# Two causal attentions in 64-row tiles with keys kept twice, and two narrow cross attentions on the halves of the rows

## What is computed

```python
# layer 0, stage l0a: 16 heads of width 8, causal
s = q @ k.T * 8 ** -0.5; s = where(key <= query, s, -big); y = softmax(s) @ v
# layer 1, stage l1a: 16 heads of width 64 on a latent of 32 values per token, causal
q_latent = (x Wq Wk_up.T) * 64 ** -0.5; s = q_latent @ latent.T; y = softmax(masked s) @ latent @ Wv_up @ Wout
# layers 2 and 3, stages l2x and l3x: 16 heads of width 8 over the 77 context tokens
s = q @ k.T * 8 ** -0.5; s = clip(s, -10000, 10000) in layer 2 only; y = softmax(s) @ v
```

## Time and profile before

| what | value |
|---|---|
| runs of the kernel before | 1514.69, 1516.36, 1518.23 us (median 1516.36) |
| profiled execution | 1514.06 us |
| its span, first to last instruction | 1512.2 us |
| mean granted clock of TensorE | 0.979 |
| VectorE, ScalarE, GpSimd busy | 63%, 45%, 23% of the span |
| DMA | 79.13 MB |

### The profile page before, as it was taken

How to read it: one execution, slowest core, us unless ns; L and a number is a source line. 1 busy time by engine, 2 the same in 40 slices (tenths; PEclk the granted TensorE clock), 3 DMA queues, 4 the chain that set the end, 5 groups by cost and what they waited for, 6 DMA issues and landing times. The chain is left out here.

```text
span 1512.2 us, 27644 instructions
## 1 busy us (share of the span) xinstructions
PE 1418.1 (94%) x10790; PEld 890.2 (59%) x10790; DVE 955.7 (63%) x1911; ACT 674.3 (45%) x1651; POOL 346.3 (23%) x372
## 2 busy tenths in 40 slices
PE   8999999999999998998998988989998999999996
PEld 6665574644666656566786857674444555664434
DVE  6676372644366655645668337668888887677755
ACT  4776244324267654524420324533556777750002
POOL 4000031100101010010421202027777665600001
PEclk9999899999899999999999999999999999999998
DMA  3000000421000000000011302010110101399980
GB/s 126 2 2 2 3 2 0 154 72 42 15 2 2 2 2 17 1 20 4 2 60 78 126 11 83 2 43 15 42 42 28 30 15 26 64 223 254 253 213 15
DMA packets 24062, 79.13 MB, mean 52 GB/s; under 512 B 4808, under 2 KB 6646, under 8 KB 23552
## 3 DMA queue, kind: packets, MB, share of 16 engines
q1 hardware_dynamic: 23072, 74.26, 18.0%
q10 hardware_dynamic: 864, 3.15, 0.8%
HBM read 72.11 MB, written 1.08 MB: 48 GB/s over the span
## 5 line engine op out<-in xcount | busy, mean ns | idle before, releaser
L193 PE MATMUL psum<-ident 128*128 128x128 f32 x1392 | 175.7, 284 | 13.0 <-DVE var L143 5.6
L193 PEld LDWEIGHTS psum<-ident 128*128 128x128 f32 x1392 | 167.4, 198 | 20.9 <-DVE var L143 6.6
L475 ACT ACTIVATE pt<-psum,quad_max 128x128 f32<-128x128 f32 (+3 forms) x256 | 133.6, 525 | 68.4 <-DVE quad_max L513 64.4
L184 POOL TENSOR_TENSOR rstd<-var,minus_half 128x4 f32<-128x4 f32 x30 | 30.7, 1023 | 574.5 <-DVE var L143 539.4
L513 DVE TENSOR_REDUCE quad_max<-psum 128x1 f32<-128x128 f32 (+3 forms) x256 | 113.5, 485 | 67.7 <-PE psum L404 67.4
L2733 PE MATMUL psum<-pt,slots 128*128 128x512 f32 x256 | 115.0, 604 | 3.5 <-DVE pt L2886 2.9
L2712 PE MATMUL psum<-slots,xn_t 128*128 128x512 f32 x256 | 113.9, 605 | 3.1 <-DVEq L2857 3.1
L2471 ACT ACTIVATE p<-psum,duo_max 128x512 f32<-128x512 f32 x128 | 86.9, 683 | 43.2 <-DVE duo_max L2506 43.1
L2801 ACT ACTIVATE pt<-psum,p 128x64 f32<-128x64 f32 x256 | 58.0, 393 | 72.5 <-POOL wide L2943 43.7
L2733 PEld LDWEIGHTS psum<-pt,slots 128*128 128x128 f32 x256 | 48.0, 192 | 69.6 <-issue 50.8
L2506 DVE TENSOR_REDUCE duo_max<-psum 128x1 f32<-128x512 f32 x128 | 82.3, 684 | 10.0 <-PE psum L2382 7.8
(11 more groups left out here) (505 smaller groups left out, 2794.1 us busy)
## 6 DMA issues: line engine op xcount, KB each, us to landing
pt<-scratch_out_gates SPq DMA_DIRECT2D x32, 256.0 KB, 12.2
heads<-scratch_out_gates SPq DMA_DIRECT2D x24, 256.0 KB, 14.5
slots<-in_s_l0f SPq DMA_DIRECT2D x8, 514.0 KB, 3.3
wide<-scratch_gates SPq DMA_DIRECT2D x8, 512.0 KB, 7.5
slots<-in_s_l3v SPq DMA_DIRECT2D x8, 512.0 KB, 3.3
context_v<-scratch_out_gates SPq DMA_DIRECT2D x16, 256.0 KB, 18.3
slots<-in_s_l3o ACTq DMA_DIRECT2D x6, 512.0 KB, 10.2
weights<-in_w_l1a SPq DMA_DIRECT2D x1, 2624.0 KB, 9.4
```

What stands on the lines that cost most here:

```text
L193: nc.tensor.matmul(m.ps[bank][:, 0:P], m.ident[:, :], m.ident[:, :], start=True, stop=True, skip_group_check=True)
L475: nc.scalar.activation(m.quad_p[:, i % 2, g, 0:keys], m.ps[g][:, 0:keys], ACT.Exp, bias=m.quad_max[:, i % 2, g:g + 1], accum_out=sum_colum ...
```

## The change

In both causal attentions:

- The keys (l0a) or latents (l1a) are kept twice, in one copy with zeros in the odd groups of 32 rows and in the other with zeros in the even ones. ScalarE writes the first copy and then VectorE the second from the same bank. Scores become matmuls over 64 rows: head place g takes the rows of half g % 2 and the copy g // 2, so the heads are in the order 0, 2, 1, 3 (`HEAD_OF`).
- The mask becomes, for each head, two bf16 matmuls over 64 rows with 64 columns each.
- The turns are in halves: rows 0 to 63 of four heads and two key blocks go to one bank, rows 64 to 127 to another. Per pair of key blocks there are two banks, VectorE copies the first and ScalarE the second. A set of 1 to 4 blocks thus uses 2, 2, 4, 4 banks, where it used 1, 2, 3, 4.
- TensorE's order becomes: scores of set i (heads 2, 3); turn of the first pair of blocks of set i - 1, after all four exponentials; scores of set i + 1 (0, 1); turn of the second pair of blocks, if there is one; values of set i - 2. VectorE's copies move likewise.

In both narrow crosses the scores are matmuls over 64 rows with `keys_own` twice as wide (616 columns to build instead of 308), and the eight transposes become sixteen halves.

Three constants are added (`later`, `parity`, `rows8`), so three DMAs and one cast on ScalarE. The core of the diff:

```diff
 def quad_scores(...):
-    for g in heads:
-        nc.tensor.matmul(m.ps[g][:, keys - P:keys], m.ident_bf[:, :], m.future_bf[:, :], start=False,
-                         stop=True).then_inc(m.quad_scores, 1)
+    for part in range(2):
+        for g in heads:
+            own, at = half_rows(g % 2), keys - P + 64 * part
+            last = nc.tensor.matmul(m.ps[g][:, at:at + 64], m.later_bf[own, part, :], m.ident_bf[own, own], start=False,
+                                    stop=part == 1)
+            if part == 1:
+                last.then_inc(m.quad_scores, 1)
+
+def quad_turn(nc, pe, m, a, n, pair):
+    banks = [turn_bank(pe, m, a.turn[n, 2 * pair + half]) for half in range(2)]
+    blocks = pair_keys(n, pair)
+    for kt in blocks:
+        for g in range(GROUP):
+            for half in range(2):
+                own, at = half_rows(half), (kt % 2 * GROUP + g) * 64
+                last = nc.tensor.transpose(banks[half][:, at:at + 64], m.quad_p[own, n % 2, g, kt * P:(kt + 1) * P],
+                                           m.ident[own, own])
+                if kt == blocks[-1] and g == GROUP - 1:
+                    last.then_inc(m.quad_turned, 1)
 
 def quad_tensor(...):
-            for kt in range(n % NQ + 1):
-                bank = turn_bank(pe, m, a.turn[n, kt])
-                for g in range(GROUP):
-                    if kt == 0:
-                        pe.wait_ge(m.quad_exp, GROUP * (a.sets0 + n) + g + 1)
-                    last = nc.tensor.transpose(bank[:, g * P:(g + 1) * P], m.quad_p[:, n % 2, g, kt * P:(kt + 1) * P],
-                                               m.ident[:, :])
-                last.then_inc(m.quad_turned, 1)
+            pe.wait_ge(m.quad_exp, GROUP * (a.sets0 + n) + GROUP)
+            quad_turn(nc, pe, m, a, n, 0)
         if i + 1 < SETS:
             quad_scores(nc, pe, m, a, i + 1, (0, 1), q, k, q_ready)
+        if 0 <= n < SETS and key_pairs(n) > 1:
+            quad_turn(nc, pe, m, a, n, 1)
...
+def quad_take(copy, eng, m, a, n, u):
+    pair, half = divmod(u, 2)
+    blocks = pair_keys(n, pair)
...
+    copy(m.quad_pt[:, n % 2, blocks[0]:blocks[-1] + 1, :].rearrange("p k (g a q) -> p (k g) a q", a=2, q=64)[:, :, half, :],
+         bank[:, 0:len(blocks) * S // 2].rearrange("p (k q) -> p k q", q=64)).then_inc(m.quad_taken[a.turn[n, u][0]], 1)
...
 def quad_vector(...):
-            for kt in range(0, n % NQ + 1, 2):
-                quad_take(nc.vector.tensor_copy, dve, m, a, n, kt)
+            quad_take(nc.vector.tensor_copy, dve, m, a, n, 0)
         if i + 1 < SETS:
             maxima(i + 1, (0, 1))
+        if 0 <= n < SETS and key_pairs(n) > 1:
+            quad_take(nc.vector.tensor_copy, dve, m, a, n, 2)
...
 def l0_attn_tensor(nc, pe, m):
-                q=lambda g, b, j, qt: m.head_qs[own(g), j, b * S + qt * P:b * S + (qt + 1) * P],
-                k=lambda g, b, keys: m.k_t[own(g), b * S:b * S + keys],
+                q=lambda g, b, j, qt: m.head_qs[half_rows(g % 2), j, b * S + qt * P:b * S + (qt + 1) * P],
+                k=lambda g, b, keys: m.head_keys[g // 2][half_rows(g % 2), b * S:b * S + keys],
...
 def l0_attn_vector(nc, dve, m):
     head_queries(0)
+    for j in range(2):
+        copied(m, dve, f"l0k{j}")
+        bank = read(m, dve, f"l0k{j}", 1)
+        nc.vector.tensor_scalar(m.head_keys[1][:, j * S:(j + 1) * S], bank[:, :], m.parity[:, 1:2], w["bk_odd"], ALU.mult,
+                                ALU.add).then_inc(emptied(m, f"l0k{j}"), 1)
...
 narrow_cross, tensor:
                 for x in range(2):
-                    rows = own(2 * half + x)
+                    rows = slice(64 * x, 64 * x + 64)
                     last = nc.tensor.matmul(m.ps[2 * (k % 2) + x][:, 0:GROUP * SC], m.q_t[rows, b * S + qt * P:b * S + (qt + 1) * P],
-                                            m.keys_own[rows, b, 0:GROUP * SC], start=True, stop=True)
+                                            m.keys_own[rows, b, half * GROUP * SC:(half + 1) * GROUP * SC], start=True, stop=True)
...
                 for h in range(8):
-                    last = nc.tensor.transpose(m.ps[4 + h // 4][0:SC, (h % 4) * P:(h % 4 + 1) * P],
-                                               m.xp[:, n % XP_BUFFERS, h * SC:(h + 1) * SC], m.ident[:, :])
+                    for low in range(2):
+                        rows = slice(64 * low, 64 * low + 64)
+                        last = nc.tensor.transpose(m.ps[4 + low][0:SC, h * 64:(h + 1) * 64],
+                                                   m.xp[rows, n % XP_BUFFERS, h * SC:(h + 1) * SC], m.ident[rows, rows])
```

More of the change, by code:

```diff
@@ L357, in __init__ @@
             if 0 <= i - 1 < SETS:
-                for kt in range((i - 1) % NQ + 1):
-                    use(self.turn, (i - 1, kt))
+                for u in range(2 * key_pairs(i - 1)):
+                    use(self.turn, (i - 1, u))
             if self.ends_group(i - 2):
@@ L373, in all_taken @@
         for bank in range(len(T_BANKS)):
-            last = max((u for (k, kt), (b, u, _) in self.turn.items() if k == n and b == bank), default=None)
+            last = max((uses for (k, _), (b, uses, _) in self.turn.items() if k == n and b == bank), default=None)
             if last is not None:
@@ L380, in quad_set, with key_pairs, pair_keys @@
     return n // (NQ * GROUP), n // NQ % GROUP, n % NQ
+def key_pairs(n):
+    return n % NQ // 2 + 1
+def pair_keys(n, pair):
+    return range(2 * pair, min(2 * pair + 2, n % NQ + 1))
 def turn_bank(pe, m, use):
@@ L466, in quad_scalar @@
         n = i - 1
-        taken = [kt for kt in range(n % NQ + 1) if kt % 2 == 1] if 0 <= n < SETS else []
+        taken = [2 * pair + 1 for pair in range(key_pairs(n))] if 0 <= n < SETS else []
         if i < SETS:
@@ L485, in quad_scalar @@
             take_output((i - 3) // a.group_sets)
-        for kt in taken:
-            quad_take(copy, act, m, a, n, kt)
+        for u in taken:
+            quad_take(copy, act, m, a, n, u)
 def quad_gpsimd(nc, pool, m, a, groups, shares, output):
@@ L548, in l0_attn_tensor @@
             nc.tensor.matmul(bank[:, :], wt, m.xn_t[:, j * S:(j + 1) * S], start=True,
-                             stop=True).then_inc(filled(m, f"{name}{j}"), 1)
+                             stop=True).then_inc(filled(m, f"{name}{j}"), 2 if name == "l0k" else 1)
     tokens_tensor(nc, pe, m, "l0v", m.xn_t, w["wv"])
-    pe.wait_ge(m.consts_cast, 2)
-    for name in ("l0q", "l0k"):
-        for j in range(2):
-            copied(m, pe, f"{name}{j}")
+    pe.wait_ge(m.consts_cast, 3)
+    for j in range(2):
+        copied(m, pe, f"l0q{j}")
+        copied(m, pe, f"l0k{j}", 1)
     def ramp(i):
@@ L1189, in l1_attn_tensor @@
     keep_busy(nc, m, 5)
-    for name in ("l1al0", "l1al1", "l1at0", "l1aq0"):
+    for j in range(2):
+        copied(m, pe, f"l1al{j}", 1)
+    for name in ("l1at0", "l1aq0"):
         copied(m, pe, name)
@@ L1242, in l1_attn_vector @@
     norm_to_turn(nc, dve, m)
+    for j in range(2):
+        copied(m, dve, f"l1al{j}")
+        bank = read(m, dve, f"l1al{j}", 1)
+        nc.vector.tensor_scalar(m.latent_t[1][:, j * S:(j + 1) * S], bank, m.parity[:, 1:2], None,
+                                ALU.mult).then_inc(emptied(m, f"l1al{j}"), 1)
     bank = read(m, dve, "l1at0")
@@ L2972, in run @@
             item(m, f"{name}{n}", 6 + n % 2)
-    for name in ("l0n", "l0q", "l0k", "l0v"):
+    for name in ("l0n", "l0q"):
         pair(name)
+    for j in range(2):
+        item(m, f"l0k{j}", 6 + j, 2)
+    pair("l0v")
     for b in range(B):
@@ L2990, in plan @@
     run("l1an", 2)
-    run("l1al", 2)
+    for j in range(2):
+        item(m, f"l1al{j}", 6 + j, 2)
     run("l1at", 1)
@@ L3090, in build @@
         m.pair_rope = heads[:, :, :].rearrange("p (s w) n -> p s w n", w=2)
-        m.latent_t = m.keys_own[:, 0, 0:T]
+        m.latent_t = [m.keys_own[:, par, 0:T] for par in range(2)]
+        m.head_keys = [m.k_t[:, :], m.wide[:, 0, :]]
         m.slots_all = sb("slots", [P, 2 * SLOT_W])
@@ L3498, in constants @@
         "future": np.where(np.arange(P)[None, :] > np.arange(P)[:, None], np.float32(-BIG), np.float32(0)),
+        "later": np.where((64 * np.arange(2)[None, :, None] + np.arange(P)[:, None, None] % 64) > np.arange(P)[None, None, :],
+                          np.float32(-BIG), np.float32(0)).reshape(P, 2 * P),
+        "parity": (np.arange(P)[:, None] // 32 % 2 == np.arange(2)[None, :]).astype(np.float32),
         "rows4": quarter * np.float32((P // H) ** -0.5),
+        "rows8": np.concatenate([quarter * (np.arange(P)[:, None] // 32 % 2 == odd) for odd in range(2)],
+                                axis=1).astype(np.float32) * np.float32((P // H) ** -0.5),
         "cols4": np.ascontiguousarray(np.broadcast_to(quarter.T[None], (P, GROUP, P))),
```

81 lines of the change are left out of this document (52 added, 29 removed).

## The result

The changed kernel takes 1498.93 us (median of four runs, 1496.50 to 1500.74) beside 1516.59 for the kernel before on the same chip: a ratio of 0.988, 95% interval 0.986 to 0.990, or -17.7 us. The forecast was -32 (1484, range 1454 to 1504): right in sign and inside its range, but nearly twice the gain. The profiled execution took 1497.48 us (span 1495.7), so -16.6 between the two traces.

The account below looks back on a forecast made before the run. TensorE's instruction stream was taken as the bound: attentions -27, starts +1.4, drains +0.6, last cross -6.0, layer 2's cross -2.2, wider keys +1.3, together -32 us from 1516.36, so 1484, range 1454 to 1504.

Parts of the forecast that it names:

- its three waits: Causal attentions, per cycle: TensorE waits 1.3 us (third tile's turn, VectorE's copy), 0.35 (fourth tile's turn), 0.45 (ScalarE's last exponential).
- The sum for a cycle: Causal attentions, four query tiles: TensorE's scores 4.27, masks 1.09, half transposes 2.72, values 2.76 plus 0.60, before waits.
- starts: Start of each causal attention: keys written twice, so the value projection begins one pass later, +0.7 us each.
- drains: Ends of the causal attentions: the halves wait for one more copy, +0.6 us in all.
- the pairs: Last narrow cross: a pair of steps falls from 5.90 to 5.04 us, 7 of 8 pairs, -6.0 us.
- the wider keys: Before both narrow crosses: masked keys twice as wide, 0.65 us more each, +1.3 in all.
- The first one: Narrow cross in layer 2, which also clips: 0.32 us saved a pair, -2.2 us over 7, before the wider keys.
- the falling clock as a rival: Causal attentions: TensorE's idle time lowers its clock; near 1600 us throughout, 1540 for half the cycles; chance 5%.
- Not held up: Rival, causal attentions: maxima and copies overlap better, a cycle is 11.4 to 12 us, kernel 1460; chance 20%.
- bind fully: Rival, causal attentions: other engines make each half cycle wait, 14.5 us a cycle, kernel 1499; chance 12%.
- (b): Causal attentions, turning the fourth tile: TensorE waits for the copy of the first part's bank, 0.35 us a cycle.
- Nothing gained: Rival: a half transpose costs 0.053 to 0.062 us instead of 0.034, kernel within 4 us of 1516; chance 3%.

Follow-up runs that it names:

- the two second traces: The kernel before and the changed kernel, each profiled once more without any edit: 1514.66 and 1500.37 us.

## Why the prediction was right, and where its sizes were off

**TensorE's instruction stream was the bound, and the other engines come last after it.** Right: the cycle, its three waits, their order and their releasers came out as walked through. The sum for a cycle was 11.4 + 2.1; it measured 11.8 + 2.09. The 0.4 is where the sum was mis-sized, and it cost 15 x 0.4 = 6 us; it is what is left of errors that partly cancel (score pairs +0.73, halves +0.26, values +0.04, masks with the entries into values -0.67). I had put the whole 0.21 us of a score pair that no column explains on the change of shape. A pair of 64 rows among 64-row tiles still has a part of it: 61.79 - 61.51 = 0.28 us at 128 columns, where the slope alone gives 0.213. That is 0.07 us that no column explains; over the cycle's eight pairs it is 0.06 to 0.11 each. Eight pairs make 0.7. The 80 halves came to some 3.0 instead of 2.72, and the masks lay, with the entries into values, at 1.0 instead of 1.7: nearer their lower bound, hidden behind the scores. That the total of the stalls came out to 0.01 is luck: its three parts are off by -0.14, +0.04 and +0.09.

**The attentions as a whole**: -17.8 us in the first trace, -25 foreseen. Cycles 15 x 1.41 = -21 (-27 foreseen); starts +0.66 and +0.88 (+0.7 each); drains +0.89 for the first, from 7.73 to 8.62 us between the last scores and the closing matmul (+0.3 each). The drains were priced as one more copy; the turns' second parts there wait 1.54 and 0.91 us, with no scores left to hide it. Between the two second traces the attentions gave 6.4 and 7.8: the clock falls behind a drain in both kernels, earlier or later.

**The crosses.** The last one: -6.0 for the pairs and +0.65 for the wider keys, together -5.35; it measured -5.74 in the first trace. That close hit is luck of the clock: it stayed up in this stage in two of ten traces only, and in the second pair of traces the stage gained 67.69 - 67.28 = 0.4 us. The prediction had no term for a falling clock there. Together with the stage behind it, which is shorter where the clock fell, the gain over all traces is 4.7. The wait ahead of TensorE's turn rose from 0.96 to 1.60 us, the 0.65 of the wider keys. The first one: -1.6 foreseen, -2.5 with the clock up, +2.1 in the trace where it fell. The prediction had put the falling clock as a rival in the attentions, with stalls of up to 1.3 us. There it did not fall within the cycles. In the cross, whose idle time I had read as harmless because ScalarE and GpSimd set the pace, a quicker TensorE left waits of 1.59 us (0.48 at the same places before), and there it did.

**The rivals.** "Not held up" (1460) fell on the three stalls, and "bind fully" (1499) has the measured total with another mechanism: (b) stayed at 0.39, the cycle at 13.9 and not 14.5. "Nothing gained" fell on 0.53 us for sixteen halves. The Trainium skill's 62 ns for each matmul, quoted in the prediction, would make these sixteen 1.0 us: this trace disagrees too. The Trainium skill states them for hardware decode off; whether it is off here no run shows.

Between the two profiled executions 32 - 16.6 = 15.4 us are missed. The stream holds 6, the starts and drains 1.3, l2x 3.7 and the untouched stages 4.9; the last cross gives 0.4 back. Of the 4.9, 2.2 in the last stage and 1.46 in the attention of layer 3 are within what the kernel before varies by (2.4 and 2.0), and the 1.25 of the cross behind l1a stay open. The medians are 1.1 nearer to the forecast. In the changed kernel's second trace the loss is spread otherwise: l2x does better than foreseen and the last cross gains almost nothing. So this account holds for one pair of executions; the cycle of 13.89 us is the part that comes back in both.

## What to carry to other kernels

When one engine's stream is shortened, walk the next engines' lists in order of time through one period: it gave three stalls to within 0.15 us in the cycle shown, and each says which instruction to try to move. Put an instruction ahead of others only if its own input is there no later than theirs: ScalarE's copy behind one more exponential brought some 9 us, VectorE's copy ahead of two maxima, whose scores were there long before, lost 60. And price the stretches where a freed engine now idles, those of stages that looked unhurried above all. Take more than one trace before a stage's time is called measured: the last cross took 62.9 us in the first trace and some 67 in most.

## What the runs showed of the hardware

A pair of 128-row masks between 64-row scores and a 64-row turn costs 0.25 us more than the same masks in 64-row products, some 0.19 of it for the change of shape (estimate above). Half transposes of 64 rows cost 0.033 us each, in pairs on the two halves.

In the cross of layer 2, TensorE's clock fell from 2.4 to 1.2 GHz (a granted clock of 0.50) behind an idle wait of 1.6 us, in a stretch where it was busy 3.41 of 5 us, in four traces of six; in the other two the same waits and the same stretch left it at 1.00. In the last cross it fell behind waits of 1.20 and 1.21 us in eight traces of ten. So the same instructions and waits can go either way. The Trainium skill, TensorE: Matmul & The Clock Gate, Part 1, section "What's actually happening", says that the window which the gate watches is free-running, and that the same kernel therefore counts a different number of slow matmuls at its start from run to run. It says this of the rise at the start; for falls later on, the 72.55 and 77.12 us of one stage in two traces of one kernel show a like difference. Filling the waits of the cross in layer 2 kept the clock up in three traces of three, and filling a drain only moved the fall to the next wait.
